# Cross attentions: attention scores from three single-pass products, with one pair of key buffers for both halves

## The chip, the cores and the metric

The kernel runs on one core of one Trainium2 chip. The metric is the device time of one execution in microseconds. TensorE (PE in the profile) does the matrix products and transposes, VectorE (DVE) and ScalarE (ACT) read its results out of PSUM, GpSimd (POOL) prepares operands in SBUF, and SyncE's queue (SP) loads from memory.

## The reference

The program is a two-layer transformer block stack on 16 sequences of 64 tokens with 256 channels. The change touches only the two cross attentions, the first and the fourth stage (names that end in `_a` and `_d`), which read a context of 1601 rows for each sequence:

```python
q = _split_heads(query @ Wq.T + bq)      # 16 heads of 16 channels
k = _split_heads(key @ Wk.T + bk)        # key and value: the context, (16, 1601, 256)
v = _split_heads(value @ Wv.T + bv)
scores = jnp.einsum('bhqd,bhkd->bhqk', q, k) / jnp.sqrt(jnp.float32(DEPTH))
scores = scores + mask * jnp.float32(-1000000000.0)
weights = jax.nn.softmax(scores, axis=-1)
ctx = jnp.einsum('bhqk,bhkd->bhqd', weights, v)
```

The first layer's attention has neither scale, bias nor mask. Between and behind the two cross attentions stand an RWKV stage, a layer of experts, a differential attention and a gated feed-forward stage; they are not changed.

## The kernel before

`cross_by_rows` does one cross attention. It works in 32 **groups** g = 2m + h: m is the sequence, h the half of the 256 channels, that is 8 of the 16 heads. The 1601 keys of a group are cut in two ways: into 4 **chunks** (three of 512 keys, one of 65) for keys and scores, and into KT = 13 tiles t of 128 keys (the last of 65) for the transposed softmax weights and the values.

For each group TensorE's program, written out as a loop over t, does the following.

- `turn(g, t)`: four transposes of a tile of softmax weights into one of two PSUM banks `turn0` and `turn1`. `move` copies the bank to SBUF, by VectorE for t = 7 to 10 (`BY_DVE`), by ScalarE for the others. `wait_moved(pe, at - 2)` holds `turn(t)` until `move(t - 2)` is done.
- `values(g, t)`: the products of the moved weights with the values.
- `scores(g + 1, c)` for chunk c of the next group: four matmuls, one for each strip of 32 rows of the array, into the four banks `scores0` to `scores3`. Chunks 1, 2, 3 stand at t = 2, 4, 6 (`ROUND_AT`), chunk 0 of the group after at t = 12. Four such matmuls are called a **round** here. Operands are plain 32-bit floats. `largest` on VectorE reads the four banks (one custom instruction each, with a read of its accumulator), adds the mask and writes `maps`.
- `k_unit(m + 1, 4h + c)` at t = 1, 4, 7, 10 (`K_AT`) and `v_unit` at t = 3, 6, 9, 11 for h = 0 and t = 3, 6, 11 for h = 1 (`V_AT`): projections of the next sequence's context. They are done in the type fp32r (one pass instead of fp32's several), as three products of upper parts and remainders (`split_products`): hi*hi, hi*lo, lo*hi. All units share one PSUM bank, `project`: `wait_bank` holds a unit until the one ahead is copied out. `keep_k` copies a key unit (ScalarE at t = 1 and 4, VectorE at t = 7 and 10), `keep_v` a value unit. The last sequence's two groups have no units behind them, so 30 of the 32 groups of a stage have them.

Each engine runs its own program strictly in the order in which it is written, and semaphores tie the engines together. GpSimd splits the context (`context`) and lays out the queries (`spread`).

Of the kernel before, what the change touches and what calls it, by code (L numbers as in the profile page):

```python
# [14 lines left out]
P = 128  # L15
# [292 lines left out]


UNIT, ROUND = unit_order(), round_order()  # L310


def cross_by_rows(nc, chip, cross, qT, attnT, loads, raw_w, wk, wv, biases, scale, mask, late, late_in, tag):
# [7 lines left out]
    with ExitStack() as ctx:  # L321
# [2 lines left out]

        def sem(name):
            return chip.sem(name + tag)
        keys = [sb(f"keys{i}", [P, KPAD]) for i in range(2)]
# [3 lines left out]
        qs = [sb(f"q_rows{i}", [P, HALVES, P]) for i in range(2)]  # L331
        parts, low = sb("max_parts", [P, 4, 4]), sb("neg_max", [P, 2, 4])
        spare = maps[1][:, :, :].rearrange("p j k -> p (j k)")
        y = spare[:, 0:NT * D].rearrange("p (n c) -> p n c", c=D)
# [7 lines left out]
        else:  # L342
# [3 lines left out]
        PJ = ctx.enter_context(nc.psum_tensor("project" + tag, [P, BANK], F32))  # L346
        OUT = ctx.enter_context(nc.psum_tensor("values" + tag, [P, HALVES, P], F32))

        set_up, q_ready, mask_in, mask_ready = (sem("set_up"), sem("q_ready"), [sem(f"mask_in{i}") for i in range(2)],
                                                sem("mask_ready"))  # L350
        k_projected, v_projected, project_free = sem("k_projected"), sem("v_projected"), sem("project_free")
# [16 lines left out]
        def bank_of(unit):  # L368
            return [PJ, TP[0], TP[1]][UNIT[unit] % 3] if UNIT[unit] < len(FIRST) else PJ

        def wait_kept(eng, unit):

            eng.wait_ge(project_free, UNIT[unit] + 1)

        def wait_moved(eng, at):

# [50 lines left out]
        @block.gpsimd  # L427
        def _(pool):
            def context(m):
                for j in range(4):  # L430
                    pool.wait_ge(v_projected, 7 * m - 7 + min(2 * j + 2, 7))
                    pool.wait_ge(k_projected, 8 * m - 8 + 4 + j + 1)
                    cross.split(pool, m, j)

            def spread(m, part):

                n = part.stop - part.start
                nc.gpsimd.tensor_tensor(
                    qs[m % 2][:, part, :].rearrange("p h (a t) -> p h a t", t=T),
                    qT[:, part, T * m:T * m + T].rearrange("p h (a t) -> p h a t", a=1).to_broadcast([P, n, 2, T]),  # L440
                    chip.cst("head_of_pair").rearrange("p (h a t) -> p h a t", h=1, t=1)
                    .to_broadcast([P, n, 2, T]), ALU.mult).then_inc(q_ready, 1)
# [36 lines left out]
            for n in range(NB - 1):  # L479
                spread_queries(n + 1)  # L480
                if masked:
                    masks(n + 1)
                if n + 2 < NB:
                    context(n + 2)

        @block.tensor
        def _(pe):
            def wait_bank(unit):
                after(pe, project_free, UNIT[unit] - 2 if UNIT[unit] < len(FIRST) else UNIT[unit])

            def k_unit(m, k):

# [21 lines left out]

            def scores(g, chunk):

                m, h, w = g // 2, g % 2, cross.width(chunk)
                if chunk == 0:
                    pe.wait_ge(q_ready, m + 2 if m or h else 1)
                wait_kept(pe, ("k", m, 4 * h + chunk))  # L520
                after(pe, score_free, ROUND["score", g, chunk, 0])
                for j in range(4):
                    own = slice(PW * j, PW * j + PW)
                    ins = nc.tensor.matmul(SC[j][:, 0:w], qs[m % 2][own, h, :],  # L524
                                           keys[h][own, BANK * chunk:BANK * chunk + w], start=True, stop=True)
                ins.then_inc(scored, 1)

            def turn(g, t):
# [69 lines left out]
                    scores(0, ROUND_BEHIND[unit])  # L598
            pe.wait_ge(set_up, 2 if masked else 3)
            pe.wait_ge(project_free, len(FIRST))  # L600
            scores(1, 0)
            for g in range(GROUPS):
                m, h = g // 2, g % 2
# [21 lines left out]
        def _(act):  # L625
            def keep_k(m, k):
                chunk, h = k % 4, k // 4
                act.wait_ge(k_projected, 8 * m + k + 1)
                after(act, scored, 4 * (2 * m + h - 1))
                nc.scalar.activation(keys[h][:, key_columns(chunk)], bank_of(("k", m, k))[:, 0:even(chunk)], ACT.Identity,  # L630
                                     bias=bk[:, h:h + 1]).then_inc(project_free, 1)

            def keep_v(m, u):
# [81 lines left out]
        def _(dve):  # L715
# [20 lines left out]
            def keep_k(m, k):  # L736
                chunk, h = k % 4, k // 4
                dve.wait_ge(k_projected, 8 * m + k + 1)
                after(dve, scored, 4 * (2 * m + h - 1))
                nc.vector.tensor_scalar(keys[h][:, key_columns(chunk)], PJ[:, 0:even(chunk)], bk[:, h:h + 1], None,  # L740
                                        ALU.add).then_inc(project_free, 1)

            def keep_v(m, u):
                dve.wait_ge(v_projected, 7 * m + u + 1)
# [53 lines left out]
            else:  # L798
                nc.vector.memset(none[:, :], 0.0).then_inc(set_up, 1)
                dve.wait_ge(set_up, 1)  # L800
            for chunk in range(4):
                for j in range(4):
# [4 lines left out]
            dve.wait_ge(bias_ready, BIASES)  # L807
# [1310 lines left out]
```

## Time and profile before

| | |
|---|---|
| median of 3 runs | 2230.22 us (2229.82 to 2231.29) |
| the profiled execution | 2230.62 us, of which the instructions span 2228.8 us |
| TensorE busy | 2029.7 us, 91% of the span |
| VectorE busy | 1226.4 us, 55% |
| ScalarE busy | 1189.3 us, 53% |
| GpSimd busy | 459.5 us, 21% |
| first cross attention (score matmuls first to last) | 25.6 to 799.4 us |
| second cross attention (the same) | 1213.7 to 1987.0 us |

The two cross attentions take about 1,550 of the 2,229 us. The profiled execution is 0.4 us above the median of the runs. A busy share tells how full an engine is on average. What sets the time in a stretch is read from which engine never waits there.

### The profile page before, as it was taken

The numbers are of one execution on the slowest core, as the hardware profiler recorded it, in microseconds if no ns is written. First come the engines' busy times: TensorE is split into PE (matmuls) and PEld (weight loads), VectorE is DVE, ScalarE is ACT, GpSimd is POOL, SyncE is SP. The second block draws the span as 40 slices with busy tenths as digits, with TensorE's granted clock in tenths as the row PEclk, the third lists the DMA queues.
The fourth block names the chain that finished last, engine by engine and source line by source line (L and its number), as shares of the span: only waits on it lengthen the run. The fifth ranks groups of instructions, "written<-read, shape, count | busy, mean of one in ns | idle before, by whom it ended". The sixth has DMA issues, their size and how long they took to land. (4 is left out here: it accounts for less than half of the span.)

```text
span 2228.8 us, 60099 instructions
## 1 busy us (share of the span) xinstructions
PE 2029.7 (91%) x25136; PEld 1574.7 (71%) x25136; DVE 1226.4 (55%) x3358; ACT 1189.3 (53%) x2297; POOL 459.5 (21%) x367
## 2 busy tenths in 40 slices
PE   6999999999999984678997999999999999987774
PEld 4777877777777762457995677777777777764443
DVE  4555555556555548834114356555555655654775
ACT  4556655665665544422322656556556665651771
POOL 3211122221112100220001333322233332200010
PEclk9999999999999997788998999999999999996867
DMA  3111111111111001003663122112122111100000
GB/s 122 42 32 31 32 32 41 41 42 32 32 32 32 7 2 57 0 9 132 225 210 103 47 56 55 46 46 72 46 56 56 46 46 51 28 2 23 1 1 26
DMA packets 68670, 110.95 MB, mean 50 GB/s; under 512 B 14505, under 2 KB 37170, under 8 KB 68402
## 3 DMA queue, kind: packets, MB, share of 16 engines
q1 hardware_dynamic: 68402, 107.10, 16.3%
q8 instruction: 201, 3.29, 0.6%
q14 instruction: 67, 0.55, 0.1%
HBM read 106.04 MB, written 1.05 MB: 48 GB/s over the span
## 5 line engine op out<-in xcount | busy, mean ns | idle before, releaser
L726 DVE CUSTOM_DVE_ANT_0 maps_d<-scores_d,mask_scaled_d 128x512 f32<-128x512 f32 (+1 forms) x512 | 263.6, 571 | 228.5 <-PE scores_d L524 228.5
L726 DVE CUSTOM_DVE_ANT_0 maps_a<-scores_a,no_mask_a 128x512 f32<-128x512 f32 (+1 forms) x512 | 263.6, 571 | 228.0 <-PE scores_a L524 228.0
L534 PE MATMUL turn_d<-const,maps_d 128*128 128x128 f32 (+1 forms) x1664 | 248.0, 280 | 0.3 <-ACT mapsT_d L644 0.3
L534 PE MATMUL turn_a<-const,maps_a 128*128 128x128 f32 (+1 forms) x1664 | 247.9, 280 | 0.3 <-ACT mapsT_a L644 0.3
L644 ACT ACTIVATE mapsT_a<-turn_a 128x512 f32<-128x512 f32 (+1 forms) x288 | 167.1, 594 | 144.8 <-PE turn_a L534 144.6
L644 ACT ACTIVATE mapsT_d<-turn_d 128x512 f32<-128x512 f32 (+1 forms) x288 | 167.0, 593 | 144.9 <-PE turn_d L534 144.6
L649 ACT ACTIVATE maps_a<-maps_a,neg_max_a 128x1024 f32<-128x1024 f32 (+1 forms) x256 | 222.5, 953 | 2.1 <-DVE neg_max_a L733 2.1
L649 ACT ACTIVATE maps_d<-maps_d,neg_max_d 128x1024 f32<-128x1024 f32 (+1 forms) x256 | 222.5, 953 | 2.1 <-DVE neg_max_d L733 2.1
L534 PEld LDWEIGHTS turn_d<-const,maps_d 128*128 128x128 f32 (+1 forms) x1664 | 185.3, 141 | 28.6 <-issue 0.9
L534 PEld LDWEIGHTS turn_a<-const,maps_a 128*128 128x128 f32 (+1 forms) x1664 | 185.2, 141 | 28.6 <-issue 0.9
L262 POOL CAST ctx_hi_a<-raw_a 128x1024 fp32r<-128x1024 f32 (+1 forms) x60 | 51.2, 853 | 525.4 <-issue 502.2
L556 PEld LDWEIGHTS values_a<-mapsT_a,v_a 128*32 128x32 f32 x6656 | 102.4, 110 | 73.4 <-issue 52.2
L556 PEld LDWEIGHTS values_d<-mapsT_d,v_d 128*32 128x32 f32 x6656 | 102.4, 110 | 73.4 <-issue 52.2
L262 POOL CAST ctx_hi_d<-raw_d 128x1024 fp32r<-128x1024 f32 (+1 forms) x60 | 51.1, 852 | 465.1 <-issue 442.0
L556 PE MATMUL values_a<-mapsT_a,v_a 128*32 128x64 f32 x6656 | 134.5, 222 | 2.8 <-ACT mapsT_a L644 2.7
L556 PE MATMUL values_d<-mapsT_d,v_d 128*32 128x64 f32 x6656 | 134.4, 222 | 2.8 <-ACT mapsT_d L644 2.7
L524 PE MATMUL scores_d<-keys_d,q_rows_d 32*128 32x512 f32 (+1 forms) x1024 | 124.2, 554 | 3.4 <-DVE max_parts_d L726 2.5
L754 DVE COPY mapsT_d<-turn_d 128x512 f32<-128x512 f32 x128 | 86.2, 686 | 74.7 <-PE turn_d L534 74.7
L754 DVE COPY mapsT_a<-turn_a 128x512 f32<-128x512 f32 x128 | 86.2, 685 | 74.4 <-PE turn_a L534 74.4
L524 PE MATMUL scores_a<-keys_a,q_rows_a 32*128 32x512 f32 (+1 forms) x1024 | 123.9, 553 | 3.4 <-DVE max_parts_a L726 2.5
L108 PE MATMUL project_a<-wv_hi_a,ctx_hi_a 128*128 128x256 f32 (+1 forms) x394 | 120.0, 305 | 0.0
L108 PE MATMUL project_d<-wv_hi_d,ctx_hi_d 128*128 128x256 f32 (+1 forms) x394 | 120.0, 305 | 0.0
(412 smaller groups left out, 4390.4 us busy)
## 6 DMA issues: line engine op xcount, KB each, us to landing
w_c<-in_L_ffn_W SPq DMA_DIRECT2D x30, 1024.0 KB, 6.8
raw_a<-in_ctxT SPq DMA_DIRECT2D x48, 512.0 KB, 3.6
raw_d<-in_ctxT SPq DMA_DIRECT2D x48, 512.0 KB, 3.7
mask_scaled_d<-in_mask SPq DMA_DIRECT2D x32, 400.2 KB, 5.5
raw_a<-in_ctxT SPq DMA_DIRECT2D x16, 65.0 KB, 2.4
raw_d<-in_ctxT SPq DMA_DIRECT2D x16, 65.0 KB, 7.0
x<-in_x SPq DMA_DIRECT2D x1, 1024.0 KB, 5.4
Wk_c_b<-in_L_attn_Wk_c SPq DMA_DIRECT2D x1, 1024.0 KB
```

The costliest lines, as they stand in the source:

```text
L108: nc.tensor.matmul(out, sh, mh, start=start, stop=False)
L262: self.nc.gpsimd.tensor_copy(self.xh[:, :, cols], self.raw[j][:, :, 0:w]).then_inc(self.ctx_hi_done, 1)
L524: ins = nc.tensor.matmul(SC[j][:, 0:w], qs[m % 2][own, h, :], keys[h][own, BANK * chunk:BANK * chunk + w], start=True, stop=True)
L534: ins = nc.tensor.transpose(TP[at % 2][0:r, P * j:P * j + P], maps[g % 2][:, j, P * t:P * t + r], chip.ident)
L556: ins = nc.tensor.matmul(OUT[PW * j:PW * j + PW, h, T * a:T * a + T], v[m % 2][0:r, PAIRS * t + 4 * h + j, 16 * a:16 * a + PW], mT[at % RI ...
L644: nc.scalar.activation(mT[at % RING][0:r, :], TP[at % 2][0:r, :], ACT.Copy).then_inc(moved_act, 1)
L649: nc.scalar.activation(maps[b][:, j, cols], maps[b][:, j, cols], ACT.Exp, bias=low[:, b, j:j + 1]).then_inc(exp_done, 1)
L726: nc.vector.tensor_tensor_reduce(maps[b][:, j, cols], SC[j][:, 0:w], mf[m % 2][:, cols] if masked else none[:, 0:w], 1.0, NEG, ALU.add, AL ...
L754: nc.vector.tensor_copy(mT[at % RING][0:r, :], TP[at % 2][0:r, :]).then_inc(moved_dve, 1)
```

## The change

Three things change in the two cross attentions.

- **Scores.** A round becomes three waves of four fp32r matmuls that add up in the same four banks: upper queries by upper keys, upper queries by key remainders, query remainders by upper keys. Twelve matmuls are issued where there were four. The narrow round has 66 columns instead of 65.
- **Keys.** `keys[0]` and `keys[1]` become `kh` and `kl` (upper part and remainder), one pair for both halves. `keep_k` writes `kh` (rounded to fp32r as it is written). A new `keep_low` on VectorE subtracts `kh` from the bank plus bias and writes `kl`. The bank is free for the next unit, and the keys for the scores, when `keep_low` is done (`keys_low`), not when `keep_k` is.
- **Queries.** `spread` on GpSimd issues three instructions instead of one: product, cast, difference.

The core of the diff:

```diff
             def spread(m, part):
...
+                pool.wait_ge(q_step, at + 1)
+                nc.gpsimd.tensor_copy(hi, q_rows[:, part, :]).then_inc(q_step, 1)
+                pool.wait_ge(q_step, at + 2)
+                nc.gpsimd.tensor_tensor(lo, q_rows[:, part, :], hi.bitcast(F32), ALU.subtract).then_inc(q_ready, 1)
...
             def wait_bank(unit):
-                after(pe, project_free, UNIT[unit] - 2 if UNIT[unit] < len(FIRST) else UNIT[unit])
+                free = UNIT[unit] - 2 if UNIT[unit] < len(FIRST) else UNIT[unit]
+                after(pe, project_free, free)
+                if free > 0 and (UNIT[unit] < len(FIRST) or BY_PLACE[free - 1][0] == "k"):
+                    after(pe, keys_low, low_keys(free))
...
-                for j in range(4):
-                    own = slice(PW * j, PW * j + PW)
-                    ins = nc.tensor.matmul(SC[j][:, 0:w], qs[m % 2][own, h, :],
-                                           keys[h][own, BANK * chunk:BANK * chunk + w], start=True, stop=True)
+                (qh, ql), cols = qs[m % 2], key_columns(chunk)
+                for stat, mov in ((qh, kh), (qh, kl), (ql, kh)):
+                    for j in range(4):
+                        own = slice(PW * j, PW * j + PW)
+                        ins = nc.tensor.matmul(SC[j][:, 0:w], stat[own, h, :], mov[own, cols],
+                                               start=stat is qh and mov is kh, stop=stat is ql, skip_group_check=True)
                 ins.then_inc(scored, 1)
...
+            def keep_low(m, k):
+
+                chunk, h, cols = k % 4, k // 4, key_columns(k % 4)
+                dve.wait_ge(project_free, UNIT["k", m, k] + 1)
+                nc.vector.scalar_tensor_tensor(kl[:, cols], bank_of(("k", m, k))[:, 0:even(chunk)], bk[:, h:h + 1],
+                                               kh[:, cols].bitcast(F32), ALU.add, ALU.subtract).then_inc(keys_low, 1)
...
                     if t in BY_DVE and t in K_AT and m + 1 < NB:
                         keep_k(m + 1, 4 * h + K_AT[t])
+                    if t in K_AT and m + 1 < NB:
+                        keep_low(m + 1, 4 * h + K_AT[t])
```

VectorE's program around t = 7 to 10 of a group with h = 1, before. `mapsT` are the targets of `move`, `turn0` and `turn1` the banks that TensorE transposes into, `project` the shared bank of the units:

```order
L754 COPY mapsT1_a<-turn0_a 128x512 [waits values_done_a,turned_a,max_ready_a]
L740 TENSOR_SCALAR keys1_a<-project_a,bk_a 128x512 [waits scored_a,k_projected_a]
L754 COPY mapsT2_a<-turn1_a 128x512 [waits values_done_a,turned_a]
L754 COPY mapsT0_a<-turn0_a 128x512 [waits values_done_a,turned_a]
L754 COPY mapsT1_a<-turn1_a 128x512 [waits values_done_a,turned_a]
L740 TENSOR_SCALAR keys1_a<-project_a,bk_a 128x66 [waits scored_a,k_projected_a]
L761 RECIPROCAL rec_a<-scores0_a 128x128 [waits out_step_a,scored_sums_a]
```

The same place in the changed kernel:

```order
L783 COPY mapsT1_a<-turn0_a 128x512 [waits values_done_a,turned_a,max_ready_a]
L762 TENSOR_SCALAR keys_hi_a<-project_a,bk_a 128x512 [waits scored_a,k_projected_a]
L769 SCALAR_TENSOR_TENSOR keys_lo_a<-project_a,bk_a,keys_hi_a 128x512 [waits project_free_a]
L783 COPY mapsT2_a<-turn1_a 128x512 [waits values_done_a,turned_a]
L783 COPY mapsT0_a<-turn0_a 128x512 [waits values_done_a,turned_a]
L783 COPY mapsT1_a<-turn1_a 128x512 [waits values_done_a,turned_a]
L762 TENSOR_SCALAR keys_hi_a<-project_a,bk_a 128x66 [waits scored_a,k_projected_a]
L769 SCALAR_TENSOR_TENSOR keys_lo_a<-project_a,bk_a,keys_hi_a 128x66 [waits project_free_a]
L790 RECIPROCAL rec_a<-scores0_a 128x128 [waits out_step_a,scored_sums_a]
```

Behind each copy of keys stands a remainder of the same size, and the move of tile 8 comes behind the first of them.

TensorE's program at t = 9 and 10 of the same group in the changed kernel, unchanged but for a wait (the first row ends `values(g, 7)`, the two `turn` pairs are tiles 9 and 10, then the sums and the key unit):

```order
L577 MATMUL values_a<-mapsT1_a,v0_a 32x64 x7
L555 MATMUL turn0_a<-const,maps1_a 128x128 [waits moved_dve_a]
L555 MATMUL turn0_a<-const,maps1_a 128x128 x3
L555 MATMUL turn1_a<-const,maps1_a 128x128 [waits moved_dve_a]
L555 MATMUL turn1_a<-const,maps1_a 128x128 x3
L564 MATMUL scores0_a<-out_copy_a,const 128x64 [waits score_free_a,out_kept_a]
L564 MATMUL scores0_a<-out_copy_a,const 128x64
L108 MATMUL project_a<-ctx_hi_a,wk_hi_a 128x66 [waits keys_low_a,project_free_a,ctx_ready_a]
```

Nothing moved here: the second `turn` still waits for VectorE's move of tile 8, and the unit behind now waits for `keys_low` as well.

## Rows read from the trace of the kernel before

**Rows 1.** The page: busy time of each engine, and the granted clock in 40 slices.

```profile
PE 2029.7 (91%) x25136; PEld 1574.7 (71%) x25136; DVE 1226.4 (55%) x3358; ACT 1189.3 (53%) x2297; POOL 459.5 (21%) x367
...
PEclk9999999999999997788998999999999999996867
```

**Rows 2.** Waits of TensorE from 60 to 700 us: total, times, longest.

```profile
PE project_a L108 <- DVE v_a L748: 0.4, 1, 0.4
```

**Rows 3.** Groups by form: busy us, mean ns, idle before.

```profile
L524 PE MATMUL scores_a<-keys_a,q_rows_a 32*128 32x512 f32 x768 | 109.5, 639 | 2.2 <-DVE max_parts_a L726 1.2 <-issue 0.8
```

**Rows 4.** Timeline of TensorE: start us, duration us; a wide and a narrow round.

```profile
306.38 0.71 PE L524 MATMUL scores_a<-keys_a,q_rows_a 32*128 32x512 f32 x4
306.38 1.14 PE L524 MATMUL scores_a<-keys_a,q_rows_a 32*128 32x512 f32 x8
307.46 0.65 PE L556 MATMUL values_a<-mapsT_a,v_a 128*32 128x64 f32 x32
...
314.75 0.45 PE L524 MATMUL scores_a<-keys_a,q_rows_a 32*128 32x65 f32 x8
315.13 0.39 PE L108 MATMUL project_a<-wv_hi_a,ctx_hi_a 128*128 128x256 f32 x1
```

**Rows 5.** One line of the kernel: duration ns minimum/median/maximum, first and last start.

```profile
L524 PE MATMUL scores_a<-keys_a,q_rows_a x1024: 270/587/692, 25.6 to 799.4; 32*128 32x512 f32 x128, 32*128 32x65 f32 x43
```

**Rows 6.** Timeline: second and sixth fp32r matmul of a wide and a narrow key unit.

```profile
304.69 0.40 PE L109 MATMUL project_a<-ctx_lo_a,wk_hi_a 128*128 128x512 f32 x1
...
305.62 0.40 PE L110 MATMUL project_a<-ctx_hi_a,wk_lo_a 128*128 128x512 f32 x1
...
323.38 0.28 PE L109 MATMUL project_a<-ctx_lo_a,wk_hi_a 128*128 128x66 f32 x1
...
323.83 0.28 PE L110 MATMUL project_a<-ctx_hi_a,wk_lo_a 128*128 128x66 f32 x1
```

**Rows 7.** Timeline: two fp32r matmuls on half the rows each, stage `_e`.

```profile
2107.45 0.51 PE L1822 MATMUL ds_e<-causal_wide_e,same_e 64*128 64x512 f32 x2 [0.35 <-ACT sc_e L1865]
2107.79 1.02 PE L1825 MATMUL ds_e<-k_block_e,q_e 64*128 64x512 f32 x4
```

**Rows 8.** Timeline, a group with h = 1: VectorE behind the key unit, transposes 9 and 10.

```profile
344.86 0.75 DVE L740 TENSOR_SCALAR keys_a<-project_a,bk_a 128x512 f32<-128x512 f32 x1 [0.66 <-PE project_a L110]
...
345.53 0.68 DVE L754 COPY mapsT_a<-turn_a 128x512 f32<-128x512 f32 x1
345.77 1.15 PE L534 MATMUL turn_a<-const,maps_a 128*128 128x128 f32 x8
```

**Rows 9.** Timeline, a group with h = 0: end of the key unit to the value unit.

```profile
319.22 0.60 PE L534 MATMUL turn_a<-const,maps_a 128*128 128x128 f32 x4
319.42 0.75 DVE L740 TENSOR_SCALAR keys_a<-project_a,bk_a 128x512 f32<-128x512 f32 x1 [0.65 <-PE project_a L110]
...
320.75 0.36 PE L108 MATMUL project_a<-wv_hi_a,ctx_hi_a 128*128 128x256 f32 x1
```

**Rows 10.** Timeline of VectorE: an instruction and the next, which waits for its result.

```profile
324.35 0.95 DVE L761 RECIPROCAL rec_a<-scores_a 128x128 f32<-128x128 f32 x1
...
325.33 0.29 DVE L763 TENSOR_TENSOR rec_a<-out_copy_a,rec_a 128x128 f32<-128x128 f32 x1
```

**Rows 11.** Groups by form: VectorE's nearest instructions with two inputs and 512 columns.

```profile
L962 DVE SCALAR_TENSOR_TENSOR mixed_b<-delta_b,mixes_b,shifted_b 128x512 f32<-128x512 f32 x20 | 13.7, 746 | 0.1
...
L860 DVE TENSOR_TENSOR x<-x,o_a 128x512 f32<-128x512 f32 x4 | 2.7, 687 | 6.7 <-PE o_a L848 6.7
```

**Rows 12.** Timeline: a wide round at t = 4, VectorE's first and last read of it.

```profile
310.48 1.14 PE L524 MATMUL scores_a<-keys_a,q_rows_a 32*128 32x512 f32 x8
...
311.80 0.69 DVE L726 CUSTOM_DVE_ANT_0 maps_a<-scores_a,no_mask_a 128x512 f32<-128x512 f32 x1 [1.56 <-PE scores_a L524]
...
314.25 0.08 DVE L726 DVE_READ_ACCUMULATOR2_ANT max_parts_a<- 128x1 f32 x1
```

**Rows 13.** Groups by form: GpSimd's idle time before its casts, and the query layout.

```profile
L262 POOL CAST ctx_hi_a<-raw_a 128x1024 fp32r<-128x1024 f32 x45 | 46.8, 1040 | 502.2 <-issue 502.2
...
L438 POOL TENSOR_TENSOR q_rows_a<-qT_a,const 128x256 f32<-128x256 f32 x15 | 9.2, 612 | 0.0
```

More of the change, by code:

```diff
@@ L310 @@
 UNIT, ROUND = unit_order(), round_order()
+BY_PLACE = list(UNIT)
 def cross_by_rows(nc, chip, cross, qT, attnT, loads, raw_w, wk, wv, biases, scale, mask, late, late_in, tag):
@@ L326, in sem @@
             return chip.sem(name + tag)
-        keys = [sb(f"keys{i}", [P, KPAD]) for i in range(2)]
+        kh, kl = sb("keys_hi", [P, KPAD], F32R), sb("keys_lo", [P, KPAD], F32R)
         v = [sb(f"v{i}", [P, KT * PAIRS, VP]) for i in range(2)]
@@ L330, in cross_by_rows @@
         mT = [sb(f"mapsT{i}", [P, BANK]) for i in range(RING)]
-        qs = [sb(f"q_rows{i}", [P, HALVES, P]) for i in range(2)]
+        qs = [[sb(f"q_{n}{i}", [P, HALVES, P], F32R) for n in ("hi", "lo")] for i in range(2)]
+        q_rows = sb("q_rows", [P, HALVES, P])
         parts, low = sb("max_parts", [P, 4, 4]), sb("neg_max", [P, 2, 4])
@@ L369, in bank_of, with low_keys @@
             return [PJ, TP[0], TP[1]][UNIT[unit] % 3] if UNIT[unit] < len(FIRST) else PJ
+        def low_keys(count):
+            return sum(kind == "k" for kind, _, _ in BY_PLACE[:count])
         def wait_kept(eng, unit):
-            eng.wait_ge(project_free, UNIT[unit] + 1)
+            if unit[0] == "k":
+                eng.wait_ge(keys_low, low_keys(UNIT[unit] + 1))
+            else:
+                eng.wait_ge(project_free, UNIT[unit] + 1)
         def wait_moved(eng, at):
@@ L435, in spread @@
             def spread(m, part):
-                n = part.stop - part.start
+                n, at = part.stop - part.start, 2 * (m + 1 if m or part.start else 0)
+                hi, lo = [t[:, part, :] for t in qs[m % 2]]
+                after(pool, q_ready, at // 2)
                 nc.gpsimd.tensor_tensor(
-                    qs[m % 2][:, part, :].rearrange("p h (a t) -> p h a t", t=T),
+                    q_rows[:, part, :].rearrange("p h (a t) -> p h a t", t=T),
                     qT[:, part, T * m:T * m + T].rearrange("p h (a t) -> p h a t", a=1).to_broadcast([P, n, 2, T]),
                     chip.cst("head_of_pair").rearrange("p (h a t) -> p h a t", h=1, t=1)
-                    .to_broadcast([P, n, 2, T]), ALU.mult).then_inc(q_ready, 1)
+                    .to_broadcast([P, n, 2, T]), ALU.mult).then_inc(q_step, 1)
+                pool.wait_ge(q_step, at + 1)
+                nc.gpsimd.tensor_copy(hi, q_rows[:, part, :]).then_inc(q_step, 1)
+                pool.wait_ge(q_step, at + 2)
+                nc.gpsimd.tensor_tensor(lo, q_rows[:, part, :], hi.bitcast(F32), ALU.subtract).then_inc(q_ready, 1)
             def spread_queries(m):
@@ L515, in scores @@
             def scores(g, chunk):
-                m, h, w = g // 2, g % 2, cross.width(chunk)
+                m, h, w = g // 2, g % 2, even(chunk)
                 if chunk == 0:
@@ L600, in _ @@
             pe.wait_ge(project_free, len(FIRST))
+            pe.wait_ge(keys_low, 8)
             scores(1, 0)
@@ L628, in keep_k @@
                 act.wait_ge(k_projected, 8 * m + k + 1)
-                after(act, scored, 4 * (2 * m + h - 1))
-                nc.scalar.activation(keys[h][:, key_columns(chunk)], bank_of(("k", m, k))[:, 0:even(chunk)], ACT.Identity,
+                after(act, scored, 4 * (2 * m + h - 1) + chunk + 1)
+                nc.scalar.activation(kh[:, key_columns(chunk)], bank_of(("k", m, k))[:, 0:even(chunk)], ACT.Identity,
                                      bias=bk[:, h:h + 1]).then_inc(project_free, 1)
@@ L738, in keep_k @@
                 dve.wait_ge(k_projected, 8 * m + k + 1)
-                after(dve, scored, 4 * (2 * m + h - 1))
-                nc.vector.tensor_scalar(keys[h][:, key_columns(chunk)], PJ[:, 0:even(chunk)], bk[:, h:h + 1], None,
+                after(dve, scored, 4 * (2 * m + h - 1) + chunk + 1)
+                nc.vector.tensor_scalar(kh[:, key_columns(chunk)], PJ[:, 0:even(chunk)], bk[:, h:h + 1], None,
                                         ALU.add).then_inc(project_free, 1)
+            def keep_low(m, k):
[3 more added lines that the diff above has]
+                                               kh[:, cols].bitcast(F32), ALU.add, ALU.subtract).then_inc(keys_low, 1)
             def keep_v(m, u):
@@ L800, in _ @@
                 dve.wait_ge(set_up, 1)
+            dve.wait_ge(bias_ready, BIASES)
+            keep_low(0, 0)
             for chunk in range(4):
+                if chunk < 3:
+                    keep_low(0, chunk + 1)
                 for j in range(4):
@@ L806, in _ @@
                 nc.vector.memset(s[:, :, 16:32], 1.0).then_inc(set_up, 1)
-            dve.wait_ge(bias_ready, BIASES)
+            for k in range(4, 8):
+                keep_low(0, k)
             for j in range(4):
```

1 line of the change is left out of this document (added).

## The prediction

> **What bounds the kernel now.** I read the page first. TensorE is busy for 91% of the span, VectorE for 55% [rows 1]. In most of the 40 slices the clock is granted at 9 tenths or more, and in the cross attentions it stays at the upper level of 2.4 GHz. The chain that ended last covers only the end of the program, so it says nothing here. The waits do: from 60 to 700 us, nearly the whole first cross attention, TensorE waited once for another engine, for 0.4 us [rows 2]. Both cross attentions are therefore bound by TensorE's own list of instructions. A nanosecond taken from that list shows in the time, and so does each new wait that holds TensorE. VectorE, ScalarE and GpSimd matter only where TensorE waits for them.
>
> **The wide round before.** It costs 1.08 us from its start at 306.38 to the next instruction at 307.46 [rows 4]. Each fp32 matmul has two records, so four matmuls are eight. The first four records end at 0.71 us, one lasts 0.692 us at most, so the four start within 0.02 us of each other: the four strips work side by side. The later four last 0.587 [rows 4, 5] and the last ends at 1.14, so it starts at 0.55 and the first of them at 0.53. The first four last 0.105 longer than the later four; I read that as the load of the first weights, which nothing hides. So half a round streams for 0.53 - 0.105 = 0.428 us, and 1.075 - 2 x 0.428 leaves 0.22 us fixed: 0.11 for the first load, 0.11 at the end, where the array goes over to another division of its rows.
>
> **The wide round after.** The three waves run in fp32r. In a wide key unit four spacings of such matmuls over 512 columns take 305.62 - 304.69 = 0.93 us, or 0.2325 each [rows 6]. Whether strips run side by side at that rate is seen for two strips of 64 rows: the pair takes 2107.79 - 2107.45 = 0.34 us, which is 0.105 for the load and 0.235 for both together [rows 7]. I take 0.2325 for four strips too. The round then costs 0.22 + 3 x 0.2325 = 0.92 us, 0.16 less. There are 768 / 8 = 96 such rounds in a stage [rows 3], 192 in both: 192 x 0.16 = **30.7 us off**. The bounds on a wave: the fp32 half round is 0.428 us for two passes, so 0.214 for one if the strips do in fp32r exactly what they do in fp32; and 0.428 if four strips at once cannot go faster than the fp32 half round, the only thing that the trace has of four strips.
>
> **The narrow round.** Before it takes 315.13 - 314.75 = 0.38 us [rows 4]. After, a wave over 66 columns streams for only 0.03 us, and the next weights take longer to load: the 66-column key unit has its matmuls 0.45 / 4 = 0.11 apart [rows 6]. So 0.105 + 2 x 0.11 + 0.03 + 0.11 = 0.465 us, 0.085 more. With 64 groups: **5.4 us on**. Per group, the rounds save 3 x 0.16 - 0.085 = 0.395 us, in all 25.3 us.
>
> **The remainders on VectorE.** The new instruction reads PSUM, adds a bias for each partition and subtracts an SBUF operand, 512 columns. The same kind of instruction with both inputs in SBUF takes 0.746 us, an addition with one input in PSUM 0.687 [rows 11]; the copy of keys that it follows takes 0.75 [rows 8]. I take 0.75, with 0.69 and 0.80 as bounds. Its average load is no matter, since VectorE is idle for nearly half of the time. What counts is whom it makes wait. VectorE's list at t = 7 is: move tile 7, copy keys, remainder, move tile 8. Two TensorE instructions wait behind.
>
> With h = 1, TensorE goes from the transposes of tile 9 straight to those of tile 10, which need move 8. Before, VectorE starts the key copy at 344.86 and move 8 at 345.53, which ends at 346.21; the transposes of tile 9 start at 345.77 and the four take 4 x 0.11 [rows 8], so those of tile 10 were due at about 346.21 and came at about 346.26. VectorE has no slack there at all. After, the remainder waits for the copy's result: a dependent instruction starts 0.03 us behind the end of the one ahead (324.35 + 0.95 to 325.33) [rows 10]. It runs from 344.86 + 0.75 + 0.03 = 345.64 to 346.39, move 8 starts 0.08 before that end, as it does behind the copy now, so at 346.31, ends at 346.99, and TensorE goes on at 347.04. **Stall: 0.78 us.**
>
> With h = 0, a value unit stands between the two transposes, and it needs the bank. The key unit has ended at 319.22, the copy starts at 319.42, and the value unit at 320.75, with no wait [rows 9]. After, the remainder ends at 319.42 + 0.75 + 0.03 + 0.75 = 320.95, and with 0.05 for the semaphore the unit starts at 321.00. **Stall: 0.25 us.** Move 8 is then late as well, but it has the value unit's 1.5 us as cover.
>
> Thirty of the 64 groups are of each kind and have units (15 in each stage): 30 x (0.78 + 0.25) = **30.9 us on**. Nothing gives this back, since TensorE is the bound before and behind.
>
> **What costs nothing.** At t = 4 the remainder stands behind VectorE's four reads of the round. Before, these start at 311.80 and the last accumulator read at 314.25, 3.77 us behind the round's start at 310.48 [rows 12]. After, they come 0.16 earlier: 3.61, then 0.04, 0.75 and 0.05 make 4.45 us. The value unit at t = 6 needs the bank 315.13 - 310.48 = 4.65 us behind the round's start now [rows 4, 12], 4.65 - 0.16 + 0.085 = 4.575 after. The margin is 0.12 us; without it each 0.1 us would cost 60 x 0.1 = 6 us. At t = 1 VectorE is free, and at t = 10 the remainder has 66 columns and ends some 0.2 us ahead of the unit behind it. GpSimd's two new instructions for each sequence, on 256 columns, are of the size of the 0.61 us layout; GpSimd idles for 502 us before its casts in one stage alone [rows 13]. In the preamble ScalarE's exponentials hold TensorE longer than the new remainders do. One pair of key buffers is enough without a wait: each chunk is read at t = 12, 2, 4, 6 and written at t = 1, 4, 7, 10, later on TensorE in each case.
>
> **Sum.** -30.7 + 5.4 + 30.9 = +5.6 us. The profiled execution took 2230.6 us, so 2236.2; the median of the runs is 0.4 lower, which gives **2236 us**. Differences below 0.2% (4.5 us) a measurement of this kernel cannot tell from none.
>
> **Rivals.**
>
> *Faster or level, because a wave streams faster.* At 0.214 us for a wave the wide round saves 0.22, 192 x 0.055 = 10.6 us more than above, and the time is 2225.5. The point at which it becomes a gain at all is a wave of 0.222 us. For it: the fp32 half rounds run at exactly that rate over four strips. Against it: all fp32r matmuls of 512 columns in the trace, the pair on two strips too, come out at 0.23.
>
> *Faster, because the remainders are hidden.* If VectorE takes both without TensorE noticing, only the rounds are left: 2230.2 - 25.3 = 2205. Against it stands VectorE's lack of slack at move 8 [rows 8].
>
> *Much slower, because four strips write four full banks at once.* The trace shows this only in fp32. If a wave took 0.428 us, the wide round would cost 1.50 us, +0.43 x 192 = +82, and with the 5.4 and 30.9 the time would be 2349; part of that is likelier than all. The Trainium skill's page "TensorE: Matmul & The Clock Gate" (Part 3) gives a measured speedup of 3.07 for four tiles of 32 rows and 512 columns, not 4. Taken as a rate, that is an estimate of 4 x 0.2325 / 3.07 = 0.303 us for a wave, a round of 1.13, and 2277 us: the rule speaks against the change. The fp32 rounds of this trace do not show such a loss, and no run here shows fp32r on four strips.
>
> *Slower by more waits.* The margin at t = 6 is lost, or a stall costs more than its wait (0.1 to 0.2 us in each of 60 groups): 2242 to 2248.
>
> **Chances.** My forecast 0.50, with its own range 2228 to 2244; waves at 0.214 or near it 0.20; remainders hidden 0.08; four strips slower 0.12; more waits 0.10. That makes faster 0.22 (the hidden remainders, half of the faster waves, and a little of the forecast's lower side), within 0.2% 0.23, slower 0.55. The range of 8 in 10 is 2218 to 2256: it leaves out the hidden remainders below and most of the slow strips above.
>
> **What the profile after would show.** A wide round of 12 records and 0.92 us to the next instruction, the narrow one 0.465. TensorE's waits, now 0.4 us, should hold about 23 us on the transposes for VectorE's moves and 7 us on the value units for the remainders, over both stages. The remainder instruction should last 0.75 us. The wrong step would be seen at once: other round lengths mean that the waves were mis-sized, other waits that VectorE's order was.

## The result and the profile after

Two sets of runs were made, each beside runs of the kernel before.

| | before, median us | after, median us | after / before, 95% interval |
|---|---|---|---|
| first set | 2230.30 (2229.82 to 2231.29, 4 runs) | 2242.06 (2238.66 to 2246.20, 4 runs) | 1.0054 (1.0041 to 1.0066) |
| second set | 2232.07 (2229.93 to 2235.41, 13 runs) | 2238.22 (2236.11 to 2243.98, 8 runs) | 1.0027 (1.0016 to 1.0038) |

The change makes the kernel slower, by 6 to 12 us. The forecast was 5.6 us slower. The profiled execution of the first set took 2238.66 us with a span of 2236.9, 8 us more than before.

The spread between runs of one kernel goes with their mean granted clock. In the second set the two runs of the changed kernel at 0.940 and 0.939 took 2242.1 and 2244.0 us, the six at 0.942 to 0.944 took 2236.1 to 2239.6. The first set ran at 0.939 to 0.941. A straight line through the runs of each kernel in the second set gives, at a clock of 0.941, some 2240.7 us after and 2233.2 before. That is an estimate of 7.5 us for the change; which of clock and time follows the other is not shown.

Page of the kernel after: busy time, and the granted clock in 40 slices.

```profile
PE 2016.8 (90%) x26160; PEld 1620.5 (72%) x26160; DVE 1386.6 (62%) x3614; ACT 1200.5 (54%) x2297; POOL 495.1 (22%) x435
...
PEclk9999999999999997788998999999999999996767
```

Against [rows 1] TensorE is 12.9 us less busy although it issues a thousand instructions more, and the span is 8.1 longer. I read from this that the waves save time and that something else makes TensorE stand. VectorE has 160 us more of work. The granted clock is 0.941 in the mean, before 0.943, and its slices differ in one digit near the end.

Kernel after, the line of the score matmuls: duration minimum/median/maximum in ns, first and last start in us. Each row is the first of the three waves; the two forms at its end are 512 and 66 columns.

```profile
L545 PE MATMUL scores_a<-keys_hi_a,q_hi_a x512: 266/492/501, 27.0 to 803.1; 32*128 32x512 f32 x128, 32*128 32x66 f32 x43
...
L545 PE MATMUL scores_d<-keys_hi_d,q_hi_d x512: 264/492/749, 1219.2 to 1995.0; 32*128 32x512 f32 x128, 32*128 32x66 f32 x43
```

From the first to the last start the first cross attention takes 803.1 - 27.0 = 776.1 us; before it took 773.8 [rows 5]. The second took 773.3 by the table ahead of the prediction; it now takes 775.8. The two stages together are 4.8 us longer; the other 3.3 us of the span lie outside them. Lengths of stages taken in this way are good to some 0.3 us: the last wave of the last round starts 0.2 to 0.3 us behind the first, and the trace's row for the second stage before ends at 1987.1 where the table has 1987.0.

Timeline of TensorE after: a narrow and a wide round, each with the instruction behind it.

```profile
316.60 0.30 PE L545 MATMUL scores_a<-keys_hi_a,q_hi_a 32*128 32x66 f32 x4
316.73 0.28 PE L545 MATMUL scores_a<-keys_lo_a,q_hi_a 32*128 32x66 f32 x4
316.84 0.28 PE L545 MATMUL scores_a<-keys_hi_a,q_lo_a 32*128 32x66 f32 x4
317.05 0.39 PE L108 MATMUL project_a<-wv_hi_a,ctx_hi_a 128*128 128x256 f32 x1
...
333.88 0.51 PE L545 MATMUL scores_a<-keys_hi_a,q_hi_a 32*128 32x512 f32 x4
334.22 0.40 PE L545 MATMUL scores_a<-keys_lo_a,q_hi_a 32*128 32x512 f32 x4
334.45 0.40 PE L545 MATMUL scores_a<-keys_hi_a,q_lo_a 32*128 32x512 f32 x4
334.77 0.65 PE L577 MATMUL values_a<-mapsT_a,v_a 128*32 128x64 f32 x32
```

They answer to [rows 4]. The wide round takes 334.77 - 333.88 = 0.89 us to the next instruction, before 1.08; the narrow one 317.05 - 316.60 = 0.45, before 0.38. The second and third wave start 334.45 - 334.22 = 0.23 apart: four strips over 512 columns stream in the time of one fp32r matmul.

TensorE's waits from 60 to 700 us.

```profile
PE turn_a L555 <- DVE mapsT_a L783: 8.1, 13, 0.6
...
PE project_a L108 <- DVE v_a L777: 0.4, 1, 0.4
```

In [rows 2] there was one wait of 0.4 us for another engine. Now there are 13 more, one in every second group: the transposes of tile 10 for VectorE's move.

Timeline of the kernel after, a group with h = 1, from the copy of keys at t = 7.

```profile
346.66 0.75 DVE L762 TENSOR_SCALAR keys_hi_a<-project_a,bk_a 128x512 fp32r<-128x512 f32 x1 [0.66 <-PE project_a L110]
...
347.44 0.75 DVE L769 SCALAR_TENSOR_TENSOR keys_lo_a<-project_a,bk_a,keys_hi_a 128x512 fp32r<-128x512 f32 x1
347.57 0.66 PE L555 MATMUL turn_a<-const,maps_a 128*128 128x128 f32 x4
...
348.11 1.28 DVE L783 COPY mapsT_a<-turn_a 128x512 f32<-128x512 f32 x2
348.85 0.66 PE L555 MATMUL turn_a<-const,maps_a 128*128 128x128 f32 x4 [0.62 <-DVE mapsT_a L783]
```

In [rows 8] the eight transposes ran as one block behind 345.77. Now tile 10's four start at 348.85, 2.19 us behind the start of the copy at 346.66; before they came 1.40 behind it (346.26 to 344.86, as worked out in the prediction). The difference is 0.79 us.

The same in a group with h = 0, to the value unit and to the key unit at t = 10.

```profile
321.34 0.75 DVE L762 TENSOR_SCALAR keys_hi_a<-project_a,bk_a 128x512 fp32r<-128x512 f32 x1 [0.65 <-PE project_a L110]
...
322.13 0.75 DVE L769 SCALAR_TENSOR_TENSOR keys_lo_a<-project_a,bk_a,keys_hi_a 128x512 fp32r<-128x512 f32 x1
322.25 0.66 PE L555 MATMUL turn_a<-const,maps_a 128*128 128x128 f32 x4
...
323.03 0.35 PE L108 MATMUL project_a<-wv_hi_a,ctx_hi_a 128*128 128x256 f32 x1
...
325.54 0.27 PE L108 MATMUL project_a<-ctx_hi_a,wk_hi_a 128*128 128x66 f32 x1
```

The value unit starts 323.03 - 321.34 = 1.69 us behind the copy's start, before 320.75 - 319.42 = 1.33 [rows 9]. That is 0.36 us, and the list of waits does not show it: the ends of matmuls are modelled, and the modelled transposes (322.25 + 0.66) reach to 0.12 us before the unit. It is seen only in the spacing of starts.

The kernel before had a wait of this hidden kind too. Its timeline, from the copy of the values to the key unit at t = 10 of the same group:

```profile
322.44 0.69 DVE L748 COPY v_a<-project_a 128x512 f32<-128x512 f32 x1 [0.72 <-PE project_a L110]
322.68 0.56 PE L543 MATMUL scores_a<-out_copy_a,const 128*128 128x64 f32 x4
...
323.28 0.27 PE L108 MATMUL project_a<-ctx_hi_a,wk_hi_a 128*128 128x66 f32 x1
```

The key unit comes 323.28 - 322.68 = 0.60 us behind the start of the sums. With h = 1, where no value unit stands ahead of it, it comes 0.36 behind them in the same trace. So some 0.24 us in each group with h = 0 went into waiting for the copy of the values, and [rows 2] does not list it. The unit starts 0.15 us behind the end of the copy.

### The profile page after: what moved, and what is told of

Read it like the earlier page. It is cut to its first block and busy times, and to the rows that moved or that the text cites. A ratio compares the mean times of both kernels' runs of the same rounds, so it can differ in the third digit from the quotient of the medians.

```text
span 2236.9 us, 62490 instructions
## 1 busy us (share of the span) xinstructions
PE 2016.8 (90%) x26160; PEld 1620.5 (72%) x26160; DVE 1386.6 (62%) x3614; ACT 1200.5 (54%) x2297; POOL 495.1 (22%) x435
## 5 line engine op out<-in xcount | busy, mean ns | idle before, releaser
L555 PEld LDWEIGHTS turn_d<-const,maps_d 128*128 128x128 f32 (+1 forms) x1664 | 185.1, 141 | 39.9 <-DVE mapsT_d L783 12.9
L555 PEld LDWEIGHTS turn_a<-const,maps_a 128*128 128x128 f32 (+1 forms) x1664 | 184.9, 141 | 39.9 <-DVE mapsT_a L783 12.9
L255 POOL TENSOR_TENSOR ctx_lo_a<-raw_a,ctx_hi_a 128x1024 fp32r<-128x1024 f32 x64 | 111.7, 1746 | 6.3 <-ACT ctx_hi_a L249 1.5
L255 POOL TENSOR_TENSOR ctx_lo_d<-raw_d,ctx_hi_d 128x1024 fp32r<-128x1024 f32 x64 | 111.9, 1748 | 4.9
```

The lines of the kernel that those rows point to most:

```text
L255: self.nc.gpsimd.tensor_tensor(self.xl[:, :, cols], self.raw[j][:, :, 0:w], self.xh[:, :, cols].bitcast(F32), ALU.subtract).then_inc(self. ...
L555: ins = nc.tensor.transpose(TP[at % 2][0:r, P * j:P * j + P], maps[g % 2][:, j, P * t:P * t + r], chip.ident)
```

## The experiments

My theory behind the result: the waves save some 25 to 29 us, and the remainder on VectorE at t = 7 gives more than that back, in two places (tile 10's transposes for h = 1, the value unit's bank for h = 0). The rivals put the loss or the gain elsewhere: four strips that stream slower, or VectorE's load as a whole.

### The waves alone

The key remainders are left out: the second wave multiplies the upper keys again, and the bank is free with the copy. The scores lack the remainder product and count the upper product twice.

```diff
-                for stat, mov in ((qh, kh), (qh, kl), (ql, kh)):
+                for n, (stat, mov) in enumerate(((qh, kh), (qh, kh), (ql, kh))):
...
-                    if t in K_AT and m + 1 < NB:
-                        keep_low(m + 1, 4 * h + K_AT[t])
```

> Three fp32r waves with the upper keys in both the first and the second wave; no remainder of keys is computed, nothing waits for one. Left out: the product of upper queries and key remainders (the upper product is added twice). My theory (VectorE's order makes TensorE wait, the rounds themselves are shorter): wide round 0.89 us, narrow 0.46, no wait of TensorE for VectorE's moves, time 2230 - 29 = 2201 us. Rival (the waves are what costs, through a slower clock or slower neighbours): 2225 us or more.

Measured: 2205.47 us (2203.36 to 2206.91), ratio 0.9879 (0.9863 to 0.9896), beside 2231.11 for the kernel before.

The score line and the waits from 60 to 700 us of this kernel:

```profile
L540 PE MATMUL scores_a<-keys_hi_a,q_hi_a x1024: 263/388/501, 26.2 to 786.3; 32*128 32x512 f32 x128, 32*128 32x66 f32 x43
L540 PE MATMUL scores_d<-keys_hi_d,q_hi_d x1024: 265/388/503, 1203.1 to 1963.6; 32*128 32x512 f32 x128, 32*128 32x66 f32 x43
```

```profile
...
PE project_a L108 <- DVE v_a L771: 0.4, 1, 0.4
```

The stages take 760.1 and 760.5 us, 26.5 less than before in all, and no wait on VectorE is added. By the medians the kernel is 25.6 us faster than the one before beside it, where I had expected 29. The waves are a gain, and the rival of slow strips is out.

### The remainders alone

One fp32 matmul for each strip as before; the copies, remainders and waits of the changed kernel stay, and the remainders are not used. The buffers are plain fp32.

```diff
-                for stat, mov in ((qh, kh), (qh, kl), (ql, kh)):
-                    for j in range(4):
...
+                for j in range(4):
+                    own = slice(PW * j, PW * j + PW)
+                    ins = nc.tensor.matmul(SC[j][:, 0:w], qh[own, h, :], kh[own, cols], start=True, stop=True)
```

> The remainder instruction and all its waits as in the changed kernel, but scores from fp32 keys in one full product as before; query and key remainders are computed and not used. My theory: wide round 1.07 us as before, stalls of 0.79 us (h = 1, transposes of tile 10) and 0.34 us (h = 0, value unit at t = 9) in 30 groups each, 34 us in all, some 2 us for the two preambles: 2266 us. Rival (the remainder is hidden and the loss comes from the waves): 2230 to 2235 us.

Measured: 2270.06 us (2269.42 to 2276.36), ratio 1.0181 (1.0164 to 1.0198); I had expected 2266.

```profile
L544 PE MATMUL scores_a<-keys_hi_a,q_hi_a x1024: 270/587/692, 27.0 to 817.8; 32*128 32x512 f32 x128, 32*128 32x66 f32 x43
L544 PE MATMUL scores_d<-keys_hi_d,q_hi_d x1024: 270/587/1214, 1234.1 to 2026.1; 32*128 32x512 f32 x128, 32*128 32x66 f32 x43
```

The score line above gives 790.8 and 792.0 us for the two stages: 35.7 more than before. The remainders cost that much by themselves. With the 26.5 of the waves the sum would be +9.2; the changed kernel's stages are 4.8 longer. Part of the difference is that the second stage began slowly here: its first round took 2.09 us in the trace, in the kernel before 1.39 (the longest matmul of the row is 1214 ns, before 951). In the first stage alone the sum is 17.0 - 13.7 = +3.3 against the +2.3 of the changed kernel. The rest I have not traced; the experiment on GpSimd below gives 14.3 for the waves in the first stage, and with it the sum is +2.7.

### The move ahead of the remainder (h = 1)

```diff
+                    if m + 1 < NB and t == 8 and h == 1:
+                        keep_low(m + 1, 4 * h + K_AT[7])
-                    if t in K_AT and m + 1 < NB:
+                    if t in K_AT and m + 1 < NB and not (t == 7 and h == 1):
                         keep_low(m + 1, 4 * h + K_AT[t])
```

> The changed kernel, but for h = 1 VectorE does the remainder of t = 7 behind the move of tile 8. My theory: the stall of 0.79 us on the transposes of tile 10 goes in all 30 groups with h = 1, 24 us less than the changed kernel: 2218 us. The stall with h = 0 stays. Rival (the wait only shifts to the next transposes, since VectorE is late by a whole instruction): within 5 us of the changed kernel, 2237 us or more.

Measured: 2219.89 us (2216.11 to 2221.03), ratio 0.9944 (0.9927 to 0.9960). I had expected 2218. It is faster than before, with every instruction of the change still there; so VectorE's load as a whole is not what costs. The timeline of a group with h = 1, and the score line:

```profile
341.90 0.68 DVE L783 COPY mapsT_a<-turn_a 128x512 f32<-128x512 f32 x1
342.15 1.15 PE L555 MATMUL turn_a<-const,maps_a 128*128 128x128 f32 x8
...
342.50 0.74 DVE L769 SCALAR_TENSOR_TENSOR keys_lo_a<-project_a,bk_a,keys_hi_a 128x512 fp32r<-128x512 f32 x1
```

```profile
L545 PE MATMUL scores_a<-keys_hi_a,q_hi_a x512: 265/492/501, 26.0 to 790.0; 32*128 32x512 f32 x128, 32*128 32x66 f32 x43
```

The eight transposes are one block again, as in [rows 8], and the remainder lies under them, since nothing needs the bank before the key unit at t = 10. The stage ran from 26.0 to 790.0 us: 764.0, 12.1 less than the changed kernel; 15 groups times 0.79 is 11.9. The second stage, 1208.1 to 1973.9 us in its row, is 10.0 shorter.

### The sums ahead of tile 10

`spread_sums` goes from t = 10 to t = 9, to stand between tile 9's transposes and whatever waits behind them, in both halves.

```diff
-                    if t == SUM_AT and g:
+                    if t == SUM_AT - 1 and g:
                         spread_sums(g - 1)
```

> The changed kernel, but TensorE spreads the sums of the last group (0.37 us of matrix work) at t = 9 instead of t = 10, ahead of the value unit (h = 0) and of the transposes of tile 10 (h = 1). My theory: this work falls into both waits, so the 0.34 us with h = 0 go and the 0.79 us with h = 1 become 0.42: 30 x (0.34 + 0.37) = 21 us less than the changed kernel, 2221 us. Rival (the waits are not where the time goes): no difference, 2242 us.

Measured: 2231.20 us (2228.80 to 2234.07), ratio 1.0002 (0.9992 to 1.0012). That is 10.9 us below the first set of the changed kernel, half of the 21 that I expected, and 7.0 below the second. The waits from 60 to 700 us, and the timeline of a group with h = 0:

```profile
PE project_a L108 <- DVE v_a L777: 5.7, 13, 0.4
PE turn_a L555 <- DVE mapsT_a L783: 3.0, 13, 0.2
```

```profile
318.55 0.66 PE L555 MATMUL turn_a<-const,maps_a 128*128 128x128 f32 x4
319.05 0.56 PE L564 MATMUL scores_a<-out_copy_a,const 128*128 128x64 f32 x4
319.41 0.36 PE L108 MATMUL project_a<-wv_hi_a,ctx_hi_a 128*128 128x256 f32 x1
...
320.91 0.60 PE L555 MATMUL turn_a<-const,maps_a 128*128 128x128 f32 x4
...
321.95 0.27 PE L108 MATMUL project_a<-ctx_hi_a,wk_hi_a 128*128 128x66 f32 x1 [0.44 <-DVE v_a L777]
```

With h = 0 the wait only moved. The sums do cover the value unit, but behind tile 10 they had been the cover of the key unit, which needs the bank that VectorE copies the values out of; it now waits 0.44 us for that. The stretch from tile 9's transposes to the key unit takes 321.95 - 318.55 = 3.40 us, in the changed kernel 325.54 - 322.25 = 3.29 (the last row of its timeline above). With h = 1 the wait shrinks from 0.62 to 0.23, and all of the gain is there: from the transposes of tile 9 to the key unit it takes 345.66 - 343.97 = 1.69 us, in the changed kernel 349.70 - 347.57 = 2.13. The stage takes 796.1 - 26.1 = 770.0 us, 6.1 less than in the changed kernel.

### Both edits

> The two edits together: in groups with h = 1 the remainder at t = 7 stands behind move 8, and the sums stand ahead of the transposes of tile 10. Theory 1 (the value unit at t = 9 of a group with h = 0 waits for the bank, and the sums there were the cover of the key unit behind it): the first edit keeps its 22 us, the second takes nothing off, since in h = 0 it lays the wait on the next unit (3.395 us instead of 3.289 for the stretch from the transposes of tile 9 to the key unit) and in h = 1 there is no wait left for it to cover; 2218 to 2223 us, as with the first edit alone. Theory 2 (each edit takes its own share off): 2220 less another 11, about 2209 us.

Measured: 2218.49 us (2215.32 to 2224.61), ratio 0.9933 (0.9918 to 0.9947), as the first edit alone. The waits from 60 to 700 us of the kernel with both:

```profile
PE project_a L108 <- DVE v_a L777: 5.7, 13, 0.4
...
```

The wait for VectorE's moves is gone and the one for the values is there, as the first theory says. The second, that each edit takes its own share off, is out.

### The remainders on GpSimd

The copy of keys writes a plain fp32 buffer of one chunk (two of them), and GpSimd makes the upper part and the remainder out of it, between its casts of the context. VectorE has no remainder in the loop, and the bank is free with the copy.

```diff
+            def split_keys(m, k):
+                chunk, h, cols = k % 4, k // 4, key_columns(k % 4)
+                pool.wait_ge(project_free, UNIT["k", m, k] + 1)
+                after(pool, scored, 4 * (2 * m + h - 1) + chunk + 1)
+                nc.gpsimd.tensor_copy(kh[:, cols], kf[k % 2][:, 0:even(chunk)]).then_inc(k_step, 1)
+                pool.wait_ge(k_step, 8 * (m - 1) + k + 1)
+                nc.gpsimd.tensor_tensor(kl[:, cols], kf[k % 2][:, 0:even(chunk)], kh[:, cols].bitcast(F32),
+                                        ALU.subtract).then_inc(keys_low, 1)
...
-                    if t in K_AT and m + 1 < NB:
-                        keep_low(m + 1, 4 * h + K_AT[t])
```

> In the loop the copy of keys writes a plain fp32 buffer, and GpSimd makes both the upper part and the remainder from it; VectorE has no remainder and the bank is free with the copy, as in the kernel before. Theory 1 (the whole loss is the two stalls at t = 7 to 10 behind the remainder on VectorE): both stalls of 0.79 and 0.34 us are gone in 30 groups each, 2242 less 34 gives 2205 to 2209 us, period of two groups 47.7 us. Rival (GpSimd's 8 more pairs of instructions for each sequence, about 0.7 and 1.4 us each, 17 us in a period of 48, delay the split context or slow VectorE by sharing SBUF): TensorE waits for ctx or keys, or VectorE's moves last longer than 0.68 us; 2215 us or more.

Measured: 2207.79 us (2203.52 to 2213.36), ratio 0.9898 (0.9879 to 0.9917). Score line, waits of TensorE from 60 to 700 us, and groups by form:

```profile
L564 PE MATMUL scores_a<-keys_hi_a,q_hi_a x512: 265/492/501, 26.6 to 786.1; 32*128 32x512 f32 x128, 32*128 32x66 f32 x43
...
L564 PE MATMUL scores_d<-keys_hi_d,q_hi_d x512: 264/492/720, 1201.1 to 1960.0; 32*128 32x512 f32 x128, 32*128 32x66 f32 x43
```

```profile
...
PE project_a L108 <- DVE v_a L800: 0.4, 1, 0.4
```

```profile
L446 POOL TENSOR_TENSOR keys_lo_a<-keys_full_a,keys_hi_a 128x512 fp32r<-128x512 f32 x81 | 103.9, 1283 | 6.5
L444 POOL CAST keys_hi_a<-keys_full_a 128x512 fp32r<-128x512 f32 x81 | 49.4, 610 | 271.8 <-ACT keys_full_a L674 196.6 <-DVE keys_full_a L785 75.1
L806 DVE COPY mapsT_a<-turn_a 128x512 f32<-128x512 f32 x128 | 86.2, 686 | 74.1 <-PE turn_a L574 74.1
```

The first stage takes 759.5 us, as with the waves alone (760.1), the second 758.9. Together they are 28.7 us shorter than in the kernel before and 33.5 shorter than in the changed kernel. So the waves take 28.7 off and the remainders on VectorE put 33.5 on. The two stalls account for 30 x (0.79 + 0.36) = 34.5 of that, and the experiment with the remainders alone gave 35.7. GpSimd's subtraction lasts 1.28 us against VectorE's 0.75 and costs nothing, since GpSimd waits for keys, not the other way round, and from 60 to 700 us TensorE never waits for it. VectorE's moves last 0.686 us, before 0.685. The Trainium skill's page "SBUF — State Buffer" (Who interferes with whom) says that a VectorE instruction with at most one SBUF input, outside its two-port modes, does not contend with GpSimd. VectorE's moves read PSUM and have no SBUF input, and their unchanged time agrees with it; in which mode they run the trace does not show.

### The narrow chunk in plain fp32

As the kernel before this, but the chunk of 65 keys is one fp32 product again, with its own small buffer.

```diff
+                if chunk == 3:
+                    for j in range(4):
+                        own = slice(PW * j, PW * j + PW)
+                        ins = nc.tensor.matmul(SC[j][:, 0:w], q_full[m % 2][own, h, :], kn[own, 0:w],
+                                               start=True, stop=True, skip_group_check=True)
```

> As the kernel with the remainders on GpSimd, and besides the narrow chunk (65 keys) goes back to one fp32 product with its own small buffer, without parts. Theory (the three waves cost more than the fp32 round where the stream is short, 0.457 against 0.381 us): 64 x 0.076 = 4.9 us less than the kernel with the remainders on GpSimd, about 2201 to 2203 us. Rival (the change of type between rounds costs something, or the next instruction hides the difference): no difference to it within 1 us.

Measured: 2205.01 us (2201.89 to 2207.04), ratio 0.9880 (0.9866 to 0.9894), 2.8 us below the kernel without this edit, with ranges that overlap; their profiled executions differ by 1.6. At the same mean granted clock, 0.938, there is one run of each: 2207.04 us here and 2211.86 there, 4.8 apart. In the timeline the narrow round is as short as in [rows 4]:

```profile
333.17 0.45 PE L568 MATMUL scores_a<-keys_narrow_a,q_rows_a 32*128 32x66 f32 x8
333.55 0.38 PE L108 MATMUL project_a<-wv_hi_a,ctx_hi_a 128*128 128x256 f32 x1
```

The sign and the round's 0.38 us are as expected. The first stage takes 756.9 us (25.8 to 782.7), 2.6 less, which is its half of the 4.9 expected; the second takes 758.3, only 0.6 less. The total is not separated from noise. This is the fastest version of the study, 27 us below the kernel before.

### The changed kernel again

> The changed kernel once more, unchanged. If the 11.8 us between the medians of before and after are the change's own, the median is again 2240 to 2243 us; if the 8 us between the profiled executions are, and the rest is spread between runs, it is 2237 to 2240 us. The start of the first round in the first cross attention should be 26.0 us where the clock has reached its upper level by then, 27.0 where it has not, in the same code.

Measured: 2238.22 us (the second set at the top). The score line:

```profile
L545 PE MATMUL scores_a<-keys_hi_a,q_hi_a x512: 263/492/501, 26.8 to 802.9; 32*128 32x512 f32 x128, 32*128 32x66 f32 x43
L545 PE MATMUL scores_d<-keys_hi_d,q_hi_d x512: 265/492/790, 1216.9 to 1994.1; 32*128 32x512 f32 x128, 32*128 32x66 f32 x43
```

The first stage takes 776.1 us, to the tenth what it took before in this kernel. What lies between the stages, which the change doesn't touch, takes 1216.9 - 802.9 = 414.0 us here and 1219.2 - 803.1 = 416.1 in the first profile of the same code; the kernel before had 1213.7 - 799.4 = 414.3. From the last score matmul to the end it is 2240.3 - 1994.1 = 246.2 here and 241.9 there. So the time outside the cross attentions differs between the two runs by 2 to 4 us; of the stages the second takes 777.2 us against 775.8, and only the first is the same in both. Behind the stages the granted clock was lower here, 0.78 from 2060 to 2120 us and 0.64 from 2120 to 2180, where the first profile has 0.81 and 0.67; in the first stage it was 1.00 in both. The first round started at 26.8, between the two values that I had named. Timeline of the first key unit, of this run and then of the first profile:

```profile
24.27 0.49 PE L109 MATMUL project_a<-ctx_lo_a,wk_hi_a 128*128 128x512 f32 x1
24.59 0.40 PE L110 MATMUL project_a<-ctx_hi_a,wk_lo_a 128*128 128x512 f32 x1
```

```profile
24.25 0.63 PE L109 MATMUL project_a<-ctx_lo_a,wk_hi_a 128*128 128x512 f32 x1
24.68 0.58 PE L110 MATMUL project_a<-ctx_hi_a,wk_lo_a 128*128 128x512 f32 x1
25.09 0.40 PE L108 MATMUL turn_a<-ctx_hi_a,wk_hi_a 128*128 128x512 f32 x1
```

In the first profile the two spacings shown are 0.43 and 0.41 us; here the one shown is already 0.32. Such matmuls later come 0.23 apart [rows 6], and this run gets there one instruction earlier than the first. The expectation put that down to the clock; the granted clock reads 1.00 from 0 to 28 us in both runs and does not show it, so only the change of spacing is shown.

## Why the prediction was right, point by point

- **Bound.** TensorE's own list is the bound: the savings in rounds and the stalls came through in the stage time. The list of waits was read too trustingly: 0.24 us for the copy of the values stood hidden in every group with h = 0, as shown above. It bore on the experiment with the sums, not on the forecast.
- **Wide round.** Predicted 0.92 us, seen 0.89, with 0.23 for a wave as taken. The stages shrink by 26.5 us where only the waves are made and by 28.7 with the remainders on GpSimd (predicted 25.3 for wide and narrow together). The rival of faster waves (0.214) did not come, nor did slow strips.
- **The rule of 3.07.** As a rate it fell. As a quotient of whole rounds it holds: twelve fp32r matmuls one after another would take 12 x 0.2325 = 2.79 us, and 2.79 / 0.89 is 3.1. About 0.2 us of the 0.89 is fixed, which I had put down to the first load and the change of row division; the streaming itself is four times as fast. The 0.303 us for a wave spread this fixed cost over the columns. The Trainium skill's page "TensorE: Matmul & The Clock Gate" (Part 3) gives 3.07 as the measured speedup of four tiles of 32 rows; the trace agrees with it over the whole round and not for the streaming.
- **Narrow round.** Predicted 0.465, seen 0.45.
- **Remainder.** Predicted 0.75 us and 0.03 behind the copy, seen 0.75 and 0.03 (346.66 + 0.75 to 347.44).
- **Stall with h = 1.** Predicted 0.78, seen 0.79, and the experiment that removes it gives 12.1 us back in one stage.
- **Stall with h = 0.** Predicted 0.25, seen 0.36. The step that was mis-sized is the 0.05 us from the remainder's end to the value unit: it ended at 322.88 and the unit started at 323.03, 0.15 behind. I had taken the 0.05 from the transposes behind a move. The trace of before had the fitting value, the key unit 0.15 behind the copy of the values. Over 30 groups this is 3 us.
- **What was to cost nothing.** The margin at t = 6 held, but it was 0.08 us and not 0.12: the remainder ends at 316.82, the value unit starts at 317.05, and 0.15 of the 0.23 between them is the hand-over. GpSimd's new instructions are hidden. The preamble was not free: the first round of the first stage now waits for the remainder of its keys (the 0.36 us below; 0.35 to 0.74 in the other kernels that have the remainder), where I had put the exponentials as cover; those come later. Timeline of the kernel after:

```profile
27.02 0.51 PE L545 MATMUL scores_a<-keys_hi_a,q_hi_a 32*128 32x512 f32 x4 [0.36 <-DVE keys_lo_a L769]
```

- **The view.** I wrote that the waits should hold some 23 and 7 us. The list has 0.62 for each of the transposes, since part of a stall lies under a modelled end, and nothing for the value units. The stalls have to be read from starts.
- **The sum.** Inside the stages +4.8 us in the first profile and +6.2 in the second, where the sum said 5.6. That it comes so near is in part luck: the rounds saved 28.7 us and not 25.3, the stalls cost 33.5 and not 30.9, and the two errors nearly cancel.
- **Outside the stages.** The prediction had nothing for this time. In the first profile 3.3 us lie here: 27.0 - 25.6 = 1.4 ahead of the first (the 0.36 among them; with the same preamble the first round starts at 26.0 in the kernel with the move ahead, so about 1 us of the 1.4 varies without a change of code), 416.1 - 414.3 = 1.8 between them, and 0.1 behind. The second profile shows that the time between and behind the stages varies by 2 and by 4 us without a change of code. The median of the first set is 4 us above that of the second, and its mean granted clock was 0.940 against 0.942; why the clock differed stays open.

## What to carry to other kernels

An instruction that is added to a half-idle engine costs what it delays on the engine that sets the time, and that is decided by its place in the list: the same 0.75 us cost 0.79 at one place, 0.36 at another and nothing one instruction later. Look first for an order in which the urgent instruction goes ahead, then for an engine that nobody waits for, even if it is slower at the work. Before an instruction is moved to cover a wait, look at what it covers where it stands.

## What the runs showed of the hardware

Four fp32r matmuls on strips of 32 rows, each into its own bank and over 512 columns, stream in 0.23 us together (334.22 to 334.45), as long as one alone over all rows (0.2325). A round of three such waves costs about 0.2 us beyond them (0.89 - 3 x 0.23). GpSimd's subtraction of two fp32 operands of 128x512 in SBUF with an fp32r result takes 1.28 us and its cast 0.61 us, and neither slows VectorE's copies out of PSUM (0.686 us with, 0.685 without). The first matmul of a unit started 0.15 us behind the end of the VectorE instruction that it waited for (323.03 behind 322.88, and 323.28 behind 323.13 in the kernel before), where a transpose started about 0.05 behind its move. Whether the shape, the type or something else makes the difference is not shown. It is not the wait for `keys_low`, which the kernel before does not have.
